# The closing stage's second low half: from VectorE to GpSimd, by way of a copy that ScalarE makes

## The reference

```python
x = x + L1_attn(layernorm(x))                 # its context arrives unnormalised, with the sums of its rows
w = where(W > d, 1, where(W < -d, -1, 0))     # d = 0.7 * mean(abs(W))
x = x + (layernorm(x) @ w.T) * alpha + bias
```

## Time and profile before

| | |
|---|---|
| median of 3 runs | 2417.37 us (2417.35 to 2419.74) |
| profiled execution, its own time | 2425.1 us |
| its span | 2423.4 us |
| mean granted clock of TensorE | 0.945 of the full 2.4 GHz |
| busy over the span | PE 90%, DVE 73%, ACT 69%, POOL 44% |
| chain that ended last, by engine | DVE 3%, PE 1%, issue 1% of the span |
| its first lines | DVE L1983 1%, DVE L2006 1%, DVE L2014 1% |

### The profile page before, as it was taken

One profiled execution on the slowest core, in us unless ns is written; L12 is line 12 of the kernel. 1 busy time (PEld: TensorE's weight loads), 2 busy tenths in 40 slices (PEclk: granted clock), 3 DMA queues, 4 the chain that ended last, 5 costly groups with the idle time before them and its releaser, 6 DMA issues. The chain is left out here.

```text
span 2423.4 us, 85735 instructions
## 1 busy us (share of the span) xinstructions
PE 2185.1 (90%) x31693; PEld 1375.4 (57%) x31693; DVE 1776.7 (73%) x5603; ACT 1664.1 (69%) x3894; POOL 1076.6 (44%) x1374
## 2 busy tenths in 40 slices
PE   6979999999967788879999995996999999999766
PEld 4643444444435676768888884563455555555354
DVE  5538999999838677744454444984999999999298
ACT  6955899899843555424454443893799999999644
POOL 3533666666654566636666664562000000000076
PEclk9987999999979899989999998997899999999888
DMA  6552333333232566745553344874232222322242
GB/s 220 203 189 75 93 91 94 94 94 93 65 97 87 146 181 185 171 115 128 141 139 96 93 89 127 267 274 147 65 80 79 81 75 81 82 74 69 64 155 95
DMA packets 363746, 290.45 MB, mean 120 GB/s; under 512 B 228400, under 2 KB 296752, under 8 KB 363344
## 3 DMA queue, kind: packets, MB, share of 16 engines
q1 hardware_dynamic: 349616, 248.24, 37.0%
q0 software_dynamic: 12960, 35.60, 4.7%
q10 hardware_dynamic: 768, 1.12, 0.2%
HBM read 133.53 MB, written 123.69 MB: 106 GB/s over the span
## 5 line engine op out<-in xcount | busy, mean ns | idle before, releaser
L765 ACT ACTIVATE a_pr<-a_pst 128x384 f32<-128x384 f32 (+3 forms) x2176 | 909.2, 486 | 112.6 <-PE a_pst L804 87.3
L804 PE MATMUL a_psc<-a_ke,a_qe 52*64 52x192 f16 (+4 forms) x6144 | 632.4, 286 | 32.5 <-DMA a_ke<-mrow 29.7
L804 PE MATMUL a_pst<-a_qe,a_ke 49*64 49x384 f16 (+5 forms) x6144 | 579.4, 288 | 1.6 <-ACT a_pr L765 0.5
L717 DVE TENSOR_REDUCE a_mx<-a_psc 128x1 f32<-128x320 f32 (+1 forms) x1152 | 537.9, 528 | 44.7 <-PE a_psc L804 36.8
L866 PE MATMUL a_po<-a_pr,a_ve 128*17 128x128 f32 (+3 forms) x10496 | 563.5, 303 | 2.0 <-ACT a_pr L765 1.1
L712 DVE CUSTOM_DVE_ANT_0 a_cut<-a_psc,row_mask 128x320 bf16<-128x320 f32 (+1 forms) x1024 | 436.3, 472 | 51.8 <-PE a_psc L804 29.6
L804 PEld LDWEIGHTS a_pst<-a_qe,a_ke 53*64 53x64 f16 (+1 forms) x6144 | 241.3, 105 | 327.9 <-ACT a_pr L765 193.9
L683 POOL TENSOR_SCALAR_AFFINE_SELECT a_pr<-a_pr 128x512 f32<-128x512 f32 x448 | 276.2, 637 | 159.4 <-ACT a_pr L765 159.4
L804 PEld LDWEIGHTS a_psc<-a_ke,a_qe 52*64 52x64 f16 (+1 forms) x6144 | 262.8, 106 | 112.1 <-DVE a_mx L717 36.3
L866 PEld LDWEIGHTS a_po<-a_pr,a_ve 128*17 128x17 f32 x10496 | 193.9, 96 | 181.9 <-issue 50.5
L663 POOL TENSOR_SCALAR a_mneg<-a_mx 128x32 f16<-128x32 f32 x64 | 18.6, 290 | 626.9 <-DVE a_mx L721 584.7
(11 more groups left out here) (242 smaller groups left out, 4168.6 us busy)
## 6 DMA issues: line engine op xcount, KB each, us to landing
a_qe<-qx SPq DMA_DIRECT2D x378, 64.0 KB, 2.7
a_ke<-kx SPq DMA_DIRECT2D x378, 64.0 KB, 2.7
vx<-p_vst SPq DMA_DIRECT2D x32, 544.0 KB, 3.3
a_ve<-vx SPq DMA_DIRECT2D x64, 272.0 KB, 3.0
qx<-p_stg SPq DMA_DIRECT2D x64, 256.0 KB, 3.4
kx<-p_stg SPq DMA_DIRECT2D x64, 256.0 KB, 3.3
ox<-a_ost SPq DMA_DIRECT2D x256, 64.0 KB
x_res<-x SPq DMA_DIRECT2D x16, 512.0 KB, 8.9
```

What stands on the lines that cost most here:

```text
L717: dve.tensor_reduce(out.unsqueeze(1), psc[(u * n_s + n) % RING][:, 0:width], AXX, ALU.max)\
L765: act.activation(pr[s % SLOTS][:, h // 2, h % 2, 0:width], pst[prob_slot(u, n) % RING][:, 0:width], ACT.Exp, scale=scale).then_inc(p_ready, 1)
L804: last = pe.matmul(out[at, col:col + count], stat[:, t * P + 64 * half:t * P + 64 * half + 64], mov[:, tok:tok + count], start=(k == 0), s ...
```

## The change

ScalarE makes, after the two high halves of a chunk, a copy of the second PSUM tile `pn[1]` in f32 in a new SBUF tile `xw`. GpSimd subtracts the second high half from it and writes the second low half. VectorE makes the first low half alone. `xw` has one buffer, so ScalarE waits with the copy until GpSimd has read the chunk before. One semaphore, `row_low`, gives way to three. The transposes into `pn[0]` now wait for VectorE's half, those into `pn[1]` for ScalarE's copy, and `product` waits for both halves. GpSimd's step stands at the end of its turn, behind `add_bias(c+1)` and `add_x(c+3)`.

```diff
+        xw = sb("xw", [P, CH], F32)
...
             def turn_rows(c):
                     if c:
-                        pe.wait_ge(row_low, EC * (c - 1) + e + 1)
+                        pe.wait_ge((low_first, row_wide)[e], c)
...
             def product(c):
-                pe.wait_ge(row_low, EC * (c + 1))
+                pe.wait_ge(low_first, c + 1)
+                pe.wait_ge(low_second, c + 1)
...
             def high(c):                                          # ScalarE
                     act.activation(xh[:, c % 2, e, :], pn[e][:, :], ACT.Copy).then_inc(row_high, 1)
+                after(act, low_second, c)
+                act.activation(xw[:, :], pn[1][:, :], ACT.Copy).then_inc(row_wide, 1)
...
+            def low(c):                                           # GpSimd
+                if c >= 2:
+                    pool.wait_ge(y_ready, 2 * (c - 1))
+                pool.wait_ge(row_high, EC * (c + 1))
+                pool.wait_ge(row_wide, c + 1)
+                pool.tensor_tensor(xl[:, c % 2, 1, :], xw[:, :], xh[:, c % 2, 1, :], ALU.subtract).then_inc(low_second, 1)
...
                 if 1 <= c + 3 < NC:
                     add_x(c + 3)
+                if 0 <= c + 1 < NC:
+                    low(c + 1)
...
             def low(c):                                           # VectorE
-                for e in range(EC):
-                    dve.wait_ge(row_high, EC * c + e + 1)
-                    dve.tensor_tensor(xl[:, c % 2, e, :], pn[e][:, :], xh[:, c % 2, e, :], ALU.subtract)\
-                       .then_inc(row_low, 1)
+                dve.wait_ge(row_high, EC * c + 1)
+                dve.tensor_tensor(xl[:, c % 2, 0, :], pn[0][:, :], xh[:, c % 2, 0, :], ALU.subtract).then_inc(low_first, 1)
```

More of the change, by code:

```diff
@@ L1804, in stage_close @@
         seen, gathered, rooted, inverted, shifted = (sem(n) for n in ("seen", "gathered", "rooted", "inverted", "shifted"))
-        normed, row_turned, row_high, row_low = sem("normed"), sem("row_turned"), sem("row_high"), sem("row_low")
+        normed, row_turned, row_high, row_wide = sem("normed"), sem("row_turned"), sem("row_high"), sem("row_wide")
+        low_first, low_second = sem("low_first"), sem("low_second")
         biased, y_ready, y_added, stored = sem("biased"), sem("y_ready"), sem("y_added"), sem("stored")
```

## The result

The changed kernel is slower: 2425.59 us (median of 7 runs) against 2418.51 for the kernel before (7 runs), ratio 1.0032, 95% interval 1.0021 to 1.0044, that is 5 to 11 us. The forecast was 2419.4 us and no change; the measured time lies 0.6 us above the range. The forecast counted +2.0 us from 2417.37, the median of the first three runs; the seven runs put the kernel before 1.1 us higher, so the change itself was forecast at +2.0 us and measured at +7.1.

A forecast was written before the change was run, and what follows sets the result against it. The prediction took VectorE as the bound before and GpSimd's queue, 6.32 us a chunk, after. Start +2.5, chunks -4.8, half-clock products +2.5 and tail +1.8 made +2.0 on 2417.37: 2419.4 us, no change, range 2413 to 2425.

The forecast's parts named there:

- the shift's coin toss: VectorE's tiny shift, before the change: slips in (0.16 us) or waits out GpSimd's second x addition (1.31 us).
- The queue of 6.32 us: GpSimd's work per chunk after the change: bias 2.75, x additions 2.44 and the low-half subtraction 1.13 us.
- the 1.36 us: GpSimd's subtraction estimated by the skill's factor: a queue of 6.52 us, some 2.6 us more over 13 chunks; not adopted.
- The start: Closing stage up to product 2: GpSimd's first low half queues behind x additions, the copy delays norm; +2.5 us.
- I take two short ones: +2.5: Chunks 2 to 13: two products with a short drop to the half clock, each costing 1.25 us.
- -4.8: Chunks 2 to 13 without half-clock products: 11 x 6.37 = 70.1 us against 74.9 before.
- the first slow rival: TensorE's clock: slower by over 4.8 us from five half-clock products on; six at 1.7 give 2424.7 us; chance 0.24.
- The prediction's own sign of being wrong: On TensorE: the prediction would be wrong if the clock were low in more than five products.
- an even chunk keeps about the idle time that it had: TensorE's idle time in even chunks, 2.3 us before, stays about the same; argued against the first slow rival.
- No coin toss any more: VectorE's shift always falls into GpSimd's first x addition and is let in at its end, some 0.6 us to spare.
- The tail: Products 13 to 15, no x additions left: 7.7 + 5.3 = 13.0 us against 11.2, so +1.8 us.
- After product 15 nothing changes: End of the closing stage, behind the last product: the change was to add no time there.

The follow-up runs named there:

- e5_before_shift: The kernel before the change, with VectorE's shift made by four one-column operations with a scalar per partition instead of one on two SBUF tensors; ratio 1.0007 to the kernel before.
- e6_fill_shift: The changed kernel with 12 extra unread multiplications on TensorE per turn and the shift in four one-column operations; ratio 0.9981 to the kernel before.
- e1_fill: The changed kernel with 12 extra unread multiplications on TensorE per turn, filling idle time before each product; ratio 1.0017 to the kernel before.
- the single edits: The changed kernel with only TensorE's 12 extra multiplications (ratio 1.0017 to the kernel before), or with only the shift in four operations (1.0025).
- e9_bias_fill_shift: The changed kernel with TensorE's extra multiplications, the shift in four operations and GpSimd's bias addition in two operations instead of four; ratio 0.9967 to the kernel before.
- e12_before_all: The kernel before, both low halves on VectorE, with extra multiplications, shift in four and bias in two; ratio 0.9996 to the kernel before.

## Why the prediction was wrong

**The bound before** was read rightly: VectorE full, with chunks of 6.3 or 7.4 us by the shift's coin toss. `e5_before_shift` took the toss away, and every chunk had one length.

**Prices.** The subtraction was taken at 1.16 us and takes 1.147 / 1.157 / 1.167; the copy at 0.59 and takes 0.60. The queue of 6.32 us was met to 0.01 in `e6_fill_shift`. The factor of about 2 that the prediction takes from the Trainium skill (GPSIMD Engine Reference, § 4.1 Engine selection), and with it the 1.36 us, does not hold for this form here: 1.157 us is 1.70 times VectorE's 0.681.

**The start** was put at +2.5 us up to product 2; the trace gives +2.2 (18.55 + 14.05 us from the first x addition, against 17.46 + 12.92).

**The step that failed** is the number of products at the half clock in "I take two short ones: +2.5". Between product 2 and 13 there are six, one in two. Their price was nearly right: a pair of chunks, one with a slow product, takes 14.16 us (7.10 + 7.06), where 2 x 6.37 + 1.25 = 13.99 was worked out. With six in place of two, the eleven chunks take 77.41 us against 74.93, +2.5 where the sum had -4.8 + 2.5 = -2.3. The two have no working of their own; they stand near the count of the kernel before (three in this stretch), as though the idle time in front of the products stayed. The prediction knew that it would be 3 us after a slow product, and did not follow that into the product after. It is a circle that keeps itself up: slow product, late copy, late norm, long chunk, idle TensorE, slow product. That was the first slow rival, given 0.24. The prediction's own sign of being wrong, a low clock in more than five products, came true with nine. What the prediction held against it, "an even chunk keeps about the idle time that it had", is where it went wrong: there was no even chunk left, and the idle time of an even chunk was no safe one, since products behind 2.13 us ran at either level before. That the rival's price for six (2424.7) comes within 1 us of the time measured is in part luck: it has six products at 1.7 us, and the profile has eight behind product 0 at about 1.2 ((6.9 + 2.9) / 8).

**The shift.** "No coin toss any more" was true of the changed kernel: every shift that met a GpSimd instruction ended with the one under way. In a queue without gaps, the state forecast, a shift can miss one end after another (`e1_fill`). Why it is let in at one end and not at another is not shown: in the changed kernel, too, x additions follow one another without a gap. With the full clock alone the steady state of 6.32 did not come; it came with both edits.

**The tail** was put at +1.8 from product 13 to 15; it is +1.0 (5.43 + 6.81 against 11.22), and then +1.2 behind product 15, which is itself at the half clock: "After product 15 nothing changes" was wrong. The first 3.4 us of products 14 and 15 after the change:

```profile
2408.90:2412.30 3.40, 3.40 (x19) 2.51 (x20) 0.83 (x2) 0.52 (x2) 2.78 (x4) 0.58 0.02 5
2415.71:2419.11 3.40, 3.29 (x16) 2.18 (x16) 0.82 (x2) 0.00 (x0) 0.00 (x0) 0.58 0.23 77
```

Together 2.2 + 2.5 + 1.0 + 1.2 = 6.9.

## What to carry to other kernels

Moving work off the full engine pays only if the next bound holds still: here the new ring ran through TensorE, which ran at the lower clock behind each 2.9 us of idle time, so a late copy bred the next late copy. Before counting on a steady state, follow one disturbed chunk through two more turns and see whether it heals; a count of slow events taken from the old kernel is no forecast for a new schedule. When one wait's removal brings less than its size, look for a second that it covered: the pair took 8.6 us off, the single edits 1.7 and 1.0.

## What the runs showed of the hardware

An operation of VectorE with two tensor operands in SBUF (128x4, 0.16 us alone) took up to 3.13 us beside GpSimd (`e1_fill`), past the ends of two GpSimd instructions that followed one another without a gap, and ended with the third. No semaphore of the program stands between the two, so the engines do not meet at semaphores only, as the start of this document has it. The same arithmetic with a scalar per partition, in four operations of 128x1, took 0.20 to 0.22 us in all of 64 cases beside the same GpSimd work (`e5_before_shift`). VectorE operations with one operand in PSUM and one in SBUF showed no such wait: the low half took 675 to 692 ns over 32 cases.

Products of 16 multiplications took 1.75 us wholly at 2.4 GHz and 3.4 wholly at 1.2, up to the transposes behind them. In the changed kernel those behind 2.9 us of idle time ran at the lower level for all or a part of their length, and those behind 1.3 at the higher. Over the eleven profiles all 22 products behind 2.89 us or more of idle time had the lower level in their first 3.4 us, in whole or in part; behind 1.61 to 2.66 us both levels occurred. On the changed kernel twelve multiplications whose result nobody reads, put into that gap, kept the higher level in every product but the first (`e1_fill`, `e6_fill_shift`, `e9_bias_fill_shift`); in `e12_before_all` product 13 fell too (0.65).
